# A decoder layer on one core: cross mask written by ScalarE, head outputs moved by DMA instead of transposed

## The reference, cut to what matters

```python
x = x + self_attention(layernorm(x))
x = x + cross_attention(layernorm(x), ctx, mask)
x = x + ffn(layernorm(x))

def cross_attention(q, ctx, mask):            # 16 heads, DK = 16
    query, key, value = heads(q @ wq.T + bq), heads(ctx @ wk.T + bk), heads(ctx @ wv.T + bv)
    scores = einsum('bhqd,bhkd->bhqk', query, key) / 4
    scores = where(mask == 0, -1e9, scores)
    return merge(softmax(scores) @ value) @ wo.T + bo
```

## Time and profile before

| | us |
|---|---|
| median of 3 runs | 1978.36 |
| profiled execution, its own time | 1985.14 |
| its span in the trace | 1983.5 |
| PE busy | 1792.5 (90%) |
| DVE busy | 1391.6 (70%) |
| ACT busy | 865.7 (44%) |
| POOL busy | 643.4 (32%) |
| DMA queue of SP, share of 16 engines | 41.5% |

### The profile page before, as it was taken

The page is one execution under the profiler, slowest core; times in us unless marked ns, Lnnn a source line. Parts: engine busy times, 40 slices in busy tenths (PEclk is TensorE's granted clock), DMA queues, the critical chain, the costliest instruction groups (busy, mean ns, idle before and its releaser), DMA issues.

```text
span 1983.5 us, 33931 instructions
## 1 busy us (share of the span) xinstructions
PE 1792.5 (90%) x12542; PEld 1036.3 (52%) x12542; DVE 1391.6 (70%) x2192; ACT 865.7 (44%) x1320; POOL 643.4 (32%) x698
## 2 busy tenths in 40 slices
PE   2879999999989999899999989999899999989897
PEld 1545555555545555555555545555555555545554
DVE  4668585785858768585885858768585786858662
ACT  3325344443444335344443544345344543544343
POOL 3241414324151251414324151252415324151300
PEclk9979999999999999999999999999999999999998
DMA  6370543725245270543725245270543725154230
GB/s 166 46 104 12 82 62 46 104 32 78 41 65 85 33 105 20 81 62 46 104 33 81 37 67 82 33 113 14 80 60 46 104 33 84 35 70 70 34 44 11
DMA packets 86606, 124.08 MB, mean 63 GB/s; under 512 B 10481, under 2 KB 53938, under 8 KB 86322
## 3 DMA queue, kind: packets, MB, share of 16 engines
q1 hardware_dynamic: 83650, 115.26, 41.5%
q0 software_dynamic: 2160, 7.87, 1.0%
q10 hardware_dynamic: 768, 0.57, 0.1%
HBM read 21.42 MB, written 8.39 MB: 15 GB/s over the span
## 4 chain that ended last, share of the span: by engine, by line
PE 56%; issue 19%; DVE 12%; POOL 6%; DMA 3%; ACT 2%; SPq 0%; POOLq 0%; ACTq 0%; DVEq 0%
PE small L1013 9%; PE o_ps L1174 7%; PE small L1237 6%; DVE negmax L746 5%; PE score L1139 5%; PE score L1096 5%; PE score L1101 4%; POOL P L469 3%; PE score L1066 3%; PE small L1268 3%; DVE xn L732 2%; DMA Q<-negT 2%; PE small L1284 2%; DVE negparts L757 2%; PE small L997 2%
## 5 line engine op out<-in xcount | busy, mean ns | idle before, releaser
L746 DVE TENSOR_REDUCE negmax<-score 128x4 f32<-128x1024 f32 (+1 forms) x448 | 538.8, 1222 | 124.9 <-PE score L1101 83.2
L570 ACT ACTIVATE P<-score 128x1024 f32<-128x1024 f32 x448 | 447.8, 1025 | 178.7 <-PE score L1116 105.1
L1174 PE MATMUL o_ps<-P,V 128*32 128x256 f32 (+1 forms) x4096 | 283.3, 363 | 25.1 <-POOL P L469 19.8
L781 DVE TENSOR_TENSOR P<-P,cross_bound 128x1024 f32<-128x1024 f32 x192 | 226.5, 1221 | 56.7 <-ACT P L570 50.8
L468 POOL TENSOR_TENSOR carrier<-minus_half 128x1 f32<-128x1 f32 x160 | 56.1, 351 | 644.4 <-ACT P L570 640.2
L1013 PE MATMUL small<-xnT,w 128*128 128x512 f32 x392 | 204.7, 665 | 5.2 <-ACT inT L527 2.7
L1096 PE MATMUL score<-K,Q 96*128 96x256 bf16 x1024 | 155.9, 274 | 56.3 <-issue 32.3
L1174 PEld LDWEIGHTS o_ps<-P,V 128*32 128x32 f32 x4096 | 86.4, 108 | 164.6 <-issue 72.8
L1139 PE MATMUL score<-Q,K 99*128 99x256 bf16 x1024 | 155.8, 275 | 7.5 <-DVE negmax L746 7.4
L408 POOL TENSOR_TENSOR rstd<-vareps,minus_half 128x4 f32<-128x4 f32 x48 | 55.0, 1146 | 307.3 <-DVE vareps L727 307.3
L1101 PE MATMUL score<-cross_q,identb 128*128 128x512 bf16 x512 | 154.2, 382 | 0.0
(11 more groups left out here) (141 smaller groups left out, 3034.4 us busy)
## 6 DMA issues: line engine op xcount, KB each, us to landing
Q<-q1p SPq DMA_DIRECT2D x96, 256.0 KB, 7.5
K<-k2p SPq DMA_DIRECT2D x96, 256.0 KB, 8.0
Q<-q2p SPq DMA_DIRECT2D x192, 128.0 KB, 5.0
x_in<-in_x SPq DMA_DIRECT2D x16, 512.0 KB, 7.8
ctxT<-in_ctx SPq DMA_DIRECT2D x16, 512.0 KB, 7.7
k2f<-q1f SPq DMA_DIRECT2D x32, 256.0 KB, 3.5
out_y<-x POOLq DMA_DIRECT2D x15, 512.0 KB, 4.8
K<-k1p SPq DMA_DIRECT2D x96, 64.0 KB, 7.3
```

What stands on the lines that cost most here:

```text
L570: A.activation(P[:, t % 4, :], score[b][:, :, :], ACT.Exp, scale=SCALE).then_inc(score_free[b], 1)
L746: V.tensor_reduce(negmax[:, k, h:h + 1024 // w], s.rearrange("p (h w) -> p h w", w=w), AX.X, ALU.max, negate=True).then_inc(score_free[b], 1)
L781: V.tensor_tensor(p, p, cross_bound[:, t % 2, :].unsqueeze(1).broadcast_to([128, 4, SEQ]), ALU.min).then_inc(probs_masked[1], 1)
L1174: last = T.matmul(o_ps[ob][32 * j:32 * j + 32, SEQ * gg + q0:SEQ * gg + SEQ], v, p, start=s == 0, stop=end, tile_position=(0, 32 * j), ski ...
```

## The change

There are two edits.

The first is the cross mask of pass one. PE's two mask matmuls of a tile go. ACT writes the mask into the score buffer ahead of the scores (`premask`), and the four score matmuls are added on top of it. The two banks `o_ps` become one tensor `o_pair`, which is a third score buffer in S2; the 16 tiles use the buffers 0, 1, 2 four times and then 0, 1, 0, 1. The first three tiles are written on ACT between `values1` and `turns(st, "xnT2_", inT)`; the rest stand among the feed-forward and part copies of S2.

The second is the way of a head's output. V's columns alternate between value and one, so that in `o_sb` the even rows hold values and the odd rows hold the sum, once per feature. Four transfers a unit (`move_heads`) bring the even rows to `oT` and the odd rows to `o_div`, 64 rows of 1 KB each. `normalise` then works in that layout: a reciprocal of 128 x 256 and a product of 128 x 256. `unit_turn`, `heads_turned` and the ACT copies of `oT` go, and their small banks with them. `oT` has a buffer of its own; `o_div` shares `q2f`.

```diff
+def premask(g, t):                                        # ACT
+    n, use = cross_use(g, t)
+    _, before = cross_tile(g, t)
+    if t == 2:
+        for ob in range(2):
+            act.wait_ge(o_free[ob], g * UNITS + UNITS // 2)
+    if positive(before):
+        act.wait_ge(score_free[n], before)
+    A.activation(cross_bufs[n][:, :, :].rearrange("p c (j k) -> p (c j) k", j=2),
+                 cross_q[:, t // 4 % 2, :].unsqueeze(1).broadcast_to([128, 4, SEQ]),
+                 ACT.Copy).then_inc(masked[n], 1)
...
+def move_heads(a, u, g):                                  # SP
+    b, gp = u // 2, u % 2
+    at = slice(SEQ * b, SEQ * b + SEQ)
+    ob, before = o_bank(a, g, u)
+    sp.wait_ge(o_free[ob], before + 1)
+    for gg in range(2):
+        rows, cols = slice(64 * gg, 64 * gg + 64), slice(SEQ * gg, SEQ * gg + SEQ)
+        sp.dma_start(oT[rows, gp, at], o_sb[0:128:2, u % 2, cols]).then_inc(o_moved[a][u], 16)
+        sp.dma_start(o_div[rows, gp, at], o_sb[1:128:2, u % 2, cols]).then_inc(o_moved[a][u], 16)
...
 def body(i, prev, nxt):                                   # SP
     if prev:
         put_neg(st, 1, 1)
+        for u in range(UNITS):
+            move_heads(1, u, i - 1)
     for b in range(GB):
         put_neg(st, 0, b)
-    for n in range(3):
-        put_part("k2", n, i)
+    for u in range(UNITS):
+        move_heads(0, u, i)
+        if u < 3:
+            put_part("k2", u, i)
...
 def unit_out(u):                                          # ACT
     act.wait_ge(pv_done, g * PVS + PV0[a] + (u + 1) * TPU[a])
     if u >= 2:
-        act.wait_ge(small_full[st.bank(name)], st.before(name) + 1)
+        act.wait_ge(o_moved[a][u - 2], 64 * (g + 1))
...
-def normalise(st, a, u, g):                               # DVE
-    dve.wait_ge(small_full[bk], st.this(f"o{a + 1}t{u}"))
-    V.reciprocal(rsum[:, u % 2, :, :], s[:, :, :, HD]).then_inc(rsum_ready[a], 1)
-    V.tensor_tensor(out, s[:, :, :, 0:HD], rsum..., ALU.mult).then_inc(free, 1)
+def normalise(a, u, g):
+    b, gp = u // 2, u % 2
+    at = slice(SEQ * b, SEQ * b + SEQ)
+    dve.wait_ge(o_moved[a][u], 64 * (g + 1))
+    chain(V.reciprocal(o_div[:, gp, at], o_div[:, gp, at]), inverse_ready[a], UNITS * g + u + 1)
+    V.tensor_tensor(oT[:, gp, at], oT[:, gp, at], o_div[:, gp, at], ALU.mult).then_inc(o_ready[a], 1)
...
 def body(i, prev, nxt):                                   # ACT
-    if prev:
-        turns(st, "oT2_", inT)
     maxima(st, 0, 0)
     exponentials(st, 0, i)
...
-    turns(st, "oT1_", oT)
...
         values1(st)
+    for t in range(3):
+        premask(i, t)
     turns(st, "xnT2_", inT)
...
-        hidden(st, range(3, HT))
+        hidden(st, range(3, HT - 2))
+    for t in range(3, N2):
+        premask(i, t)
+        if prev and t in (5, 8):
+            hidden(st, [HT - 2 + (t - 5) // 3])
+        if nxt and t == 6:
+            part("q1", 0, whole, part1, i + 1)
+        if nxt and t == 7:
+            part("k1", 0, whole, part1, i + 1)
+        if t == 12:
+            maxima(st, 1, 0)
+        if nxt and t == 13:
+            part("q1", 1, rest1, part2, i + 1)
+        if nxt and t == 14:
+            part("k1", 1, rest1, part2, i + 1)
+        if prev and t == 14:
+            ffn_out(st, 0)
...
 def cross_scores(g, tiles):                               # PE
-    pe.wait_ge(score_free[n], before)
+    pe.wait_ge(masked[n], use + 1)
...
-    for c in range(2):
-        last = T.matmul(score[n][:, c, :], identb[:, :], again(cross_q[:, k % 2, :], 2), ...)
...
 def body(i, prev, nxt):                                   # PE
-    unit_turn(st, 1, i - 1, 3)
-    heads_turned(st, 1)
-    copied(st, "oT2_")
-    tokens(st, "out2", inT, wo2, 0, 0)
+    pe.wait_ge(o_ready[1], UNITS * (i - 1) + 2)
+    tokens(st, "out2", oT, wo2, 0, 0)
...
-    unit_turn(st, 0, i, 3)
-    heads_turned(st, 0)
-    copied(st, "oT1_")
     for r in range(2):
+        pe.wait_ge(o_ready[0], UNITS * i + 2 * r + 2)
         tokens(st, "out1", oT, wout, r)
```

More of the change, by code:

```diff
@@ L257, in layer @@
         N1, N2 = GB * 6, GB * 8
-        TILE0 = {"S1": 0, "E1": N1, "S2": 2 * N1, "E2": 2 * N1 + N2}
-        TILES = 2 * N1 + 2 * N2
+        CROSS_BUF = [0, 1, 2] * 4 + [0, 1, 0, 1]
+        CROSS_USES = [CROSS_BUF.count(n) for n in range(3)]
+        assert CROSS_USES[0] == CROSS_USES[1]
+        TILE0 = {"S1": 0, "E1": N1, "E2": 2 * N1 + 2 * CROSS_USES[0]}
+        TILES = 2 * N1 + 2 * CROSS_USES[0] + N2
         PV0 = {0: 0, 1: N1}
@@ L279, in tile, with cross_use, cross_tile @@
             return n % 2, g * (TILES // 2) + n // 2
+        def cross_use(g, t):
+            n = CROSS_BUF[t]
+            return n, g * CROSS_USES[n] + CROSS_BUF[:t].count(n)
+        def cross_tile(g, t):
+            n, use = cross_use(g, t)
+            return (n, use) if n == 2 else (n, g * (TILES // 2) + N1 + CROSS_BUF[:t].count(n))
         def o_bank(a, g, u):
@@ L377, in _ @@
             put_neg(END, 1, 1)
+            for u in range(UNITS):
+                move_heads(1, u, NG - 1)
             for r in range(2):
@@ L560, in unit_out @@
                     if u >= 2:
-                        name = f"o{a + 1}t{u - 2}"
-                        act.wait_ge(small_full[st.bank(name)], st.before(name) + 1)
-                    A.activation(o_sb[:, u % 2, :], o_ps[b][:, :], ACT.Copy).then_inc(o_free[b], 1)
+                        act.wait_ge(o_moved[a][u - 2], 64 * (g + 1))
+                    elif a == 1:
+                        act.wait_ge(o_moved[0][u + 2], 64 * (g + 1))
+                    elif positive(g):
+                        act.wait_ge(o_moved[1][u + 2], 64 * g)
+                        act.wait_ge(small_full[st.bank("out2_1")], st.this("out2_1"))
+                    A.activation(o_sb[:, u % 2, :], o_ps[b], ACT.Copy).then_inc(o_free[b], 1)
                 for t in range(n):
@@ L692, in _ @@
             exponentials(END, 1, NG - 1)
-            for b in range(GB):
-                bk = END.bank(f"oT2_{b}")
-                act.wait_ge(small_full[bk], END.this(f"oT2_{b}"))
-                bank, free = small[bk], small_free[bk]
-                A.activation(inT[:, :, SEQ * b:SEQ * b + SEQ], bank[:, :].rearrange("p (c q) -> p c q", c=NC),
-                             ACT.Copy).then_inc(free, 1)
             turns(END, "xnT3_", xnT3)
@@ L736, in row_max @@
             def row_max(a, g, t):
-                b, before = tile(("S1", "S2")[a], g, t)
+                b, before = tile("S1", g, t) if a == 0 else cross_tile(g, t)
                 dve.wait_ge(score_full[b], before + 1)
-                s = score[b][:, :, :].rearrange("p c n -> p (c n)")
+                s = cross_bufs[b][:, :, :].rearrange("p c n -> p (c n)")
                 if a == 0 and t % 6 >= 4:
@@ L749, in cut_max @@
             def cut_max(a, g, t, b):
-                for last in (t, t - 1):
-                    n, before = tile(("S1", "S2")[a], g, last)
+                for last in (t, t - 1) if a == 0 else (t, t - 1, 5 if b == 0 else 11):
+                    n, before = tile("S1", g, last) if a == 0 else cross_tile(g, last)
                     dve.wait_ge(score_free[n], before + 1)
@@ L904, in body @@
                     if prev and t in (1, 4):
-                        normalise(st, 1, 2 if t == 1 else 3, i - 1)
+                        normalise(1, 2 if t == 1 else 3, i - 1)
                     if t == 5:
@@ L1089, in cross_scores @@
                     b = k // 2
-                    n, before = tile("S2", g, t)
-                    if positive(before):
-                        pe.wait_ge(score_free[n], before)
+                    n, use = cross_use(g, t)
+                    pe.wait_ge(masked[n], use + 1)
                     for c in range(2):
```

123 lines of the change are left out of this document (37 added, 86 removed).

## The result

| | before | after |
|---|---|---|
| median, us | 1979.09 | 2315.27 |
| runs | 4 | 4 (2312.85 to 2319.75) |
| span of the profiled execution | 1983.5 | 2311.2 |
| mean granted TensorE clock | 0.98 | 0.857 |

The ratio is 1.1702, with a 95% interval of 1.168 to 1.1723: the change makes the kernel 336 us slower. I had forecast 2220 us and a range up to 2300. The sign and the places were right, the size was too small.

The account below looks back on a forecast made before the run. PE was taken as the bound, DVE right behind. Terms 4.3 + 5.5 + 2.4 (masks) + 0 (S2) + 3.5 (clock) made 15.7 us a body, 241 in all on the profiled 1985.1: forecast 2220 us, range 2070 to 2300.

Parts of the forecast that it names:

- What bounds the kernel: Whole body: PE sets the pace, busy 109.2 of 117.5 us, with DVE right behind in E2, S1 and S2.
- The reciprocal: DVE's normalise: 256 columns take 1.67 us, so a unit takes 1.5 us more, eight times a body.
- The rival of a cheap one: DVE's normalise: reciprocal as cheap as a product, 0.5 us; +100 to +125 us in all, 2090 us; chance 0.17.
- A: E2 and S1: transfer wait and longer reciprocals put DVE's last `cut_max` 4.3 us later a body.
- B: E1 and D: unit transfers queue among K2's copies, so `latent` moves 9.8 us, +5.5 beyond the E2 and S1 delay.
- E1 on PE starts behind DVE's last maxima, about 2.9 us late: Start of E1: PE's work and the unit copies with it come about 2.9 us late.
- unit 1 (256 KB, 1.1 us) 803.5: Queue in E1 and D: unit 1 lands at 803.5, 1.1 us after part 0's three copies end at 802.4.
- The masks in D: D: three ACT masks of 1.0 us in a 0.6 us gap make `query2` and all behind it 2.4 us later.
- S2 even: S2: saved PE mask work and ACT's mask writes come out even, 0 us, bounds -1.2 and +3.
- my price per tile: S2: PE needs 0.88 us a tile instead of 1.31, so DVE's 1.24 is the floor; at most 1.0 us won.
- C: D: PE's idling brings the half clock, so `latent` and half of `out1` take twice as long, +3.5 us, bounds 0 and 8.
- rival 2: TensorE's clock stays up, all else as forecast: 12.2 us a body, 2165 us; chance 0.2.

Follow-up runs that it names:

- K2's copies last: The changed kernel with SP issuing all four self units ahead of the six copies of K2's parts: 2205.46 us, ratio 1.1132.
- no reciprocal: The changed kernel with a copy of 128 x 256 in place of the reciprocal, so no division is done: 2205.94 us, ratio 1.1133.
- both: The changed kernel with the four self units issued before K2's copies and a copy in place of the reciprocal: 2078.1 us, ratio 1.0494.
- both, masks late: The changed kernel with self units before K2's copies, a copy for the reciprocal, and the first masks after ACT's copies `inT`: 2045.95 us, ratio 1.0341.
- after, masks late: The changed kernel with two of the first three masks after ACT's copies `inT`, the third after hidden tile 2: 2269.34 us, ratio 1.1454.
- after, filler: The changed kernel with seven unread matmuls a body on PE, four ahead of hidden tile 0, three ahead of `latent`: 2282.64 us, ratio 1.1537.
- The last run: Kernel before plus third score buffer; ACT writes only that buffer's masks, PE the others; 44 fulfilled waits ahead of the loop: 1938.94 us, ratio 0.98.

## Why the prediction was wrong in size

| kernel | S1 to S2 | S2 to S1 | body | median |
|---|---|---|---|---|
| before | 74.9 | 44.2 | 119.1 | 1979 |
| after | 92.3 | 47.7 | 140.0 | 2315 |
| K2's copies last | 85.4 | 47.8 | 133.1 | 2205 |
| no reciprocal | 87.6 | 45.2 | 132.8 | 2206 |
| both | 80.6 | 45.1 | 125.3 | 2078 |
| both, masks late | 77.8 | 45.1 | 122.9 | 2046 |
| after, masks late | 89.2 | 47.3 | 136.5 | 2269 |
| after, filler | 90.3 | 47.5 | 137.8 | 2283 |

1. **What bounds the kernel** was read rightly. The 13.4 us of PE work a body bought nothing. For the mask half a run shows it: 6.9 us of matmuls less, the masks placed well, and still 1990 us for 1981.
2. **The reciprocal**: 1.67 us forecast, 1.75 measured. The rival of a cheap one fell, and the 2.1 us that I had worked out from the Trainium skill, VectorE: DVE Perf Modes (Walkthrough: the 8-slice pipeline in each mode), were too long.
3. **A, E2 and S1**: +4.3 forecast, +7.0 measured. E2 was nearly right: the first maximum of S1 comes 3.0 us later, for 2.5. S1 adds 4.1 for 1.8. Its two reciprocals are 1.5 us each, as priced, but I set 0.61 + 0.6 us of earlier waits against them, and a new one took their place: 1.58 us for the transfer of the third cross unit, since `times_v` and so ACT's copy were late themselves.
4. **B, E1 and D**: +5.5 forecast, +8.8 measured. The mechanism is shown: with K2's copies last, 6.9 us a body go. Two steps of it failed. The first is "E1 on PE starts behind DVE's last maxima, about 2.9 us late". It came as late as those maxima did, 7.1 us: ACT's copy of the first unit starts 54.2 us into the body (775.52), for 47.1 before (788.98). And 2.9 was less than my own A of 4.3. The second is "unit 1 (256 KB, 1.1 us) 803.5", 7.1 us behind the landing of unit 0. It took 8.9 (780.05 to 788.90), and no row shows a rate of 256 KB in 1.1 us; the stretch moved 114 to 150 GB/s. From there to unit 3 the forecast held, 8.7 us for 8.6. These steps are the whole miss of 6.0 us at `latent`: 4.2 for the late start, of which 2.7 are A's, and 1.8 for unit 1. ACT's wait of 6.07 us for the landing of unit 1, too, was not in the forecast. I had looked for who reads `o_sb`'s transfers, not for who wants the buffer back. But unit 3 landed 3.1 us behind unit 2 where I had put 3.3, so that wait is no part of the miss; what it costs by itself no run shows. The prediction's 2.6 us a unit, from the Trainium skill, DMA: Bandwidth & Descriptors (Anatomy of one DMA), go by a fit that the page gives for single transfers issued by gpsimd; a unit here is four of SP's.
5. **The masks in D**: +2.4 forecast, 2.1 measured for the copies `inT`. That `hidden(2)` then runs at half clock is 1.8 us more against the body that I read, but in twelve bodies of before it mostly does so too (3.2 us in the median, for 3.6). Taken together, placing them later was worth 3.1 to 3.3 us.
6. **S2 even**: 0 forecast, 0 measured, for the mix that I had named: ACT's masks eat what PE is spared. But "at most 1.0 us is won" was wrong for the stage with another mix. The last run wins 2.9 there: two buffers don't carry PE over DVE's cut, which my price per tile had left out, and PE, busy for 21.0 of the 23.0 us, was as near the bound as DVE.
7. **C, the clock**: +3.5 forecast, for `latent` and half of `out1`. `latent` lost 1.8 as priced, `out1` only 0.5, since the clock came back within it, and `hidden(2)`, which had no term, 1.8. The filler gave 2.2 us a body back, and rival 2 (the clock stays up) fell.
8. **The sum**: 15.7 forecast; 7.0 + 8.8 + 2.1 + 2.3 + 1.8 = 22.0 of the 22.4 us by which this body is longer. A and B, short by 2.7 and 3.3, are the failed terms. Over typical bodies the miss is 20.9 - 15.7 = 5.2 us, 73 us in 14 bodies. The first body, too, has the whole queue of E1 and D and the masks: from its first maximum of S1 to the next body's it went from 111.1 to 130.0 us, 18.9 more where I had put 5. With 13.9 there, that is 87 of the 95 us by which the forecast missed.

Left open: the last 67 us of the kernel with all three edits (2046 for 1979), 3.8 a body. The transfers' own time and the half clock at `latent` (1077 ns a matmul) are there, but no run splits them. And no run shows why the mask edit's loop is loaded again with 940 instructions ahead of it and not with 1004.

## What to carry to other kernels

When a copy through PSUM and PE is replaced by a transfer, list what the queue issues ahead of it, count from when its producer will really be done, and ask also who waits to reuse the buffer that it reads. Such a wait returns one queue later and on another engine, 6.07 us here. Work taken from PE can come back as clock, since PE stands where it had been busy. Before an edit's time is believed, compare the packets of the instruction queue, for the place of a loop's code can cost more than the edit; and split an edit with two ideas in it, for here a third buffer with four masks on ACT was worth 2%, and was hidden under twelve masks more on ACT and transfers in the wrong order.

## What the runs showed of the hardware

- DVE's reciprocal on fp32 costs 1751 ns for 128 x 256 and 253 ns for 128 x 16: 6.2 ns a column, six times a product's.
- ACT writes 128 x 1024 fp32 to PSUM in 1020 ns.
- A loop on PE of 1612 instructions (in the trace) was loaded again at each of its 13 jumps back, with 9 packets of 16 KB and 8.6 us of standing still, and with 64 instructions more ahead of it was not: 2172 and 2040 us.
- A transfer of 64 KB landed after 2.1 us in the median, and 5.8 us after its last issue behind three of 256 KB.
- Useless matmuls in TensorE's waits raised the mean granted clock by 0.03 both times, and made one kernel 33 us faster and the other no different.
